# Taking the waits between indirect transfers out of a mixture-of-experts scatter and gather

## The reference

```python
probs = sigmoid(x @ router_w.T + expert_bias)      # 160 experts
top_w, top_idx = top_k(probs, 8)
top_w = 2.5 * top_w / (sum(top_w) + 1e-9)
h1 = silu(einsum('th,eih->eti', x, w_gate))         # 64 wide
routed = einsum('eti,ehi->th', h1 * combine.T[:, :, None], w_down)
out = routed + silu(x @ w_gate_shared.T) @ w_down_shared.T
```

## Time and profile before

| what | value |
|---|---|
| median of 3 runs | 2990.82 us (2987.16 to 2993.22) |
| profiled execution | 2990.82 us, of which the span of the core's instructions is 2989.0 us |
| PE busy | 1635.8 us, 55% |
| DVE busy | 1358.2 us, 45% |
| POOL busy | 1076.5 us, 36% |
| ACT busy | 951.4 us, 32% |
| granted TensorE clock, mean | 0.730 |
| moved by indirect transfers | 67.17 MB of 352.97 MB |

### The profile page before, as it was taken

The page is one execution under the profiler, slowest core; times in us unless marked ns, Lnnn a source line. Parts: engine busy times, 40 slices in busy tenths (PEclk is TensorE's granted clock), DMA queues, the critical chain, the costliest instruction groups (busy, mean ns, idle before and its releaser), DMA issues. The chain is left out here.

```text
span 2989.0 us, 40678 instructions
## 1 busy us (share of the span) xinstructions
PE 1635.8 (55%) x14020; PEld 1134.2 (38%) x14020; DVE 1358.2 (45%) x3644; ACT 951.4 (32%) x1757; POOL 1076.5 (36%) x1177
## 2 busy tenths in 40 slices
PE   3864411782555553355078445554313468888885
PEld 2543401562343443244056334342112333554454
DVE  3548820421223346667042112335433465766755
ACT  3641100331222241131033122222576532443444
POOL 1001555445444355565544454444551110000001
PEclk9985555896777765565579777676657776989998
DMA  8991112894666511211189656661110000000001
GB/s 235 260 397 48 37 40 81 294 327 148 215 205 205 180 50 38 57 39 38 43 270 327 209 185 212 191 210 58 38 37 11 1 1 1 2 1 2 1 2 29
DMA packets 276794, 352.97 MB, mean 118 GB/s; under 512 B 68625, under 2 KB 161105, under 8 KB 276433
## 3 DMA queue, kind: packets, MB, share of 16 engines
q10 hardware_dynamic: 83984, 153.13, 15.3%
q1 hardware_dynamic: 159840, 130.08, 14.6%
q0 software_dynamic: 32768, 67.17, 7.5%
HBM read 201.35 MB, written 167.51 MB: 123 GB/s over the span
## 5 line engine op out<-in xcount | busy, mean ns | idle before, releaser
L2033 POOL DMA_INDIRECT slot_rows<-arena,SLOTS x512 | 509.9, 996 | 558.1 <-DMA slot_rows<-arena,SLOTS 314.6
L2048 POOL DMA_INDIRECT arena<-slot_results,SLOTS x512 | 491.8, 961 | 525.6 <-issue 301.1
L1994 DVE COPY arena<-psum 128x512 f32<-128x512 f32 x288 | 194.5, 689 | 694.0 <-PE psum L2268 586.1
L2091 ACT ACTIVATE arena<-psum 128x512 f32<-128x512 f32 x288 | 171.9, 597 | 940.5 <-issue 384.4
L2219 PE MATMUL psum<-ident,arena 128*128 128x128 f32 x1152 | 222.7, 325 | 321.9 <-DMA arena<-slot_rows 321.9
L2268 PE MATMUL psum<-arena 64*128 64x128 f32 x2304 | 245.8, 341 | 259.3 <-DVE arena L1994 216.6
L2010 DVE SCALAR_TENSOR_TENSOR X<-arena,WEIGHTS,X 128x128 f32<-128x128 f32 x512 | 179.9, 352 | 355.4 <-DMA arena<-slot_results,SLOTS 339.2
L2268 PEld LDWEIGHTS psum<-arena 64*128 64x128 f32 x2304 | 184.6, 223 | 320.2 <-issue 289.1
L2219 PEld LDWEIGHTS psum<-ident,arena 128*128 128x128 f32 x1152 | 144.1, 161 | 365.5 <-issue 200.4
L2258 PE MATMUL psum<-arena 128*64 128x128 f32 x2304 | 219.0, 318 | 43.8 <-issue 43.0
L169 POOL TENSOR_SCALAR rstd<-mv 128x4 f32<-128x4 f32 x32 | 6.8, 212 | 610.0 <-DVE mv L581 609.7
(11 more groups left out here) (253 smaller groups left out, 3043.6 us busy)
## 6 DMA issues: line engine op xcount, KB each, us to landing
arena<-slot_rows ACTq DMA_DIRECT2D x288, 256.0 KB
slot_results<-arena ACTq DMA_DIRECT2D x288, 256.0 KB
arena<-expert_blocks SPq DMA_DIRECT2D x512, 96.0 KB
slot_rows<-zeros SPq DMA_DIRECT2D x2, 18432.0 KB, 80.0
arena<-own_blocks SPq DMA_DIRECT2D x44, 256.0 KB
slot_rows<-arena,SLOTS POOLq DMA_INDIRECT x512
arena<-slot_results,SLOTS POOLq DMA_INDIRECT x512
expert_blocks<-in_expert_w SPq DMA_DIRECT2D x1, 7680.0 KB, 26.1
```

Of the source, the lines that this page charges most:

```text
L1994: dve.tensor_copy(YSB[:, p].rearrange("p (c h) d -> p h c d", h=2), psum[:, first:first + 2, 0:256].rearrange("p h (c d) -> p h c d", c=2) ...
L2033: pool.indirect_dma_start(out=slot_rows[h], out_offset=bass.IndirectOffsetOnAxis(ap=slots_of(t, k), axis=0), in_=XNH[:, t], in_offset=None ...
L2048: pool.indirect_dma_start(out=GATHERED[:, n % TPI, k], out_offset=None, in_=slot_results[h], in_offset=bass.IndirectOffsetOnAxis(ap=slots_ ...
L2091: act.activation(XSBT[:, g % 2], psum[:, g % 2, :], ACT.Copy).then_inc(c_xt.sem, 1)
```

## The change

The four waits that pace POOL inside `dispatch` and `gather` are deleted. The waits for a tile's inputs stay (`e_xn`, `s_idx`, and `g_sum` for a free buffer), and so do the waits of ACT for a whole scatter, of POOL for all stores ahead of a gather, and of DVE for all 8 transfers of the tile that it sums.

```diff
             for t in range(HTILES * h, HTILES * h + HTILES):
                 pool.wait_ge(e_xn.sem, e_xn.at(run, t // TPI))
                 pool.wait_ge(s_idx.sem, s_idx.at(run, t // TPI))
-                if t % HTILES:
-                    pool.wait_ge(d_rows[h][(t - 1) % TPI].sem, d_rows[h][(t - 1) % TPI].at(run, (t - 1) % HTILES // TPI))
                 stand(pool)
                 for k in range(TOPK):
-                    if k == TOPK // 2:
-                        pool.wait_ge(d_rows[h][t % TPI].sem, d_rows[h][t % TPI].at(run, t % HTILES // TPI, 16 * k))
                     pool.indirect_dma_start(...)
...
             for n in range(HTILES * h, HTILES * h + HTILES):
                 pool.wait_ge(g_sum.sem, g_sum.at(run, n - TPI))
-                if n % HTILES:
-                    pool.wait_ge(g_rows[(n - 1) % TPI].sem, g_rows[(n - 1) % TPI].at(run, (n - 1) // TPI))
                 stand(pool)
                 for k in range(TOPK):
-                    if k == TOPK // 2:
-                        pool.wait_ge(g_rows[n % TPI].sem, g_rows[n % TPI].at(run, n // TPI, 16 * k))
                     pool.indirect_dma_start(...)
```

## The result

The kernel after takes 3177.22 us (median of 4 runs, 3172.23 to 3184.66), the kernel before 2990.13 (4 runs, 2987.16 to 2993.22): a ratio of 1.0628 [1.0602, 1.0653], 6.3% slower where 15% faster was forecast. The profiled execution took 3171.14 us, its span is 3169.2.

What follows compares the result with a forecast made beforehand. POOL's stream of indirect transfers, idling at the deleted waits, was taken to set the end. Stage gains summed to 462 us off a 2989.0 us span, giving 2527, or 2529 us with 1.8 around it; eight-in-ten range 2465 to 2730.

Steps and rivals of the forecast that it cites:

- The unit: Cost of one indirect transfer on POOL without the waits: 1.30 us a scatter, 1.26 us a gather.
- S1: First scatter stage, no expert stage beside it: 128 scatters would take 166.2 us; gain 51.5 us.
- E1, S2: First expert stage beside the second scatter stage: next expert loads could start after 201.5 us, not 258.3; gain 57.
- E2, G1: Second expert stage beside the first gather stage: 211 us instead of 287.5, DVE hardly waiting for gathers; gain 76.5.
- G2 and S3: Second gather and third scatter stages: third expert stage's loads 342 us after the gather stage's start, not 440; gain 98.
- E3, S4: Third expert stage beside the fourth scatter stage: 201.5 us instead of 259.3; gain 57.8.
- E4, G3: Fourth expert stage beside the third gather stage: 211 us instead of 286.6; gain 75.6.
- G4 and the rest: Last gather stage and mamba recurrence: ACT's three waits, 50.4 us, nearly vanish and ACT becomes the bound; gain 46.
- The third: Rival: DVE's work stretches packed transfers to 2.43 us each, making the kernel slower, 3503 us; chance 0.05.
- the long E1: Sign of being wrong: the first expert stage taking well over 200 us.
- The first: Rival: stages beside expert stages do not shrink because DMA backlog replaces the waits; 267 us lost, 2796 us; chance 0.15.
- The second: Rival: the wait moves into POOL's transfer instructions, which grow to the present pitch; nothing changes, 2991 us; chance 0.05.

Runs made afterwards that it cites:

- calm512_crowd768: Kernel after, plus POOL memsets before every second transfer: 512 elements in stages without an expert stage beside them, 768 in the others; 2631.92 us, ratio to before 0.8825.
- the memset part: Part of a kernel without the model: DVE and ACT pass a semaphore while POOL runs 96 memsets back to back; 1.17 us a round, 0.45 with POOL idle.
- hop: Kernel without the model: DVE and ACT pass a semaphore beside various POOL work; 1.40 us a round under scatters without waits, 0.47 with the waits of before.
- queue: Kernel without the model: DVE and ACT pass a token beside unpaced scatters, with extra copies or PE multiplies; delayed rounds 1.40 us, 7.00 with four more DVE copies.
- the ring: Kernel without the model: a token goes round DVE, ACT, PE and SP beside scatters with various pauses; 5.60 us a round without pauses, 0.76 with both landing waits.
- window4: Kernel after, with a wait before each transfer for the landing of the fourth one before it; 3152.62 us.

## Why the prediction was wrong

**The step that failed** is in "The unit": "waiting for landings only idles POOL", and with it the choice of 1.30 and 1.26 us for a transfer whatever stands beside it. I had named what the trace did not show, a run of more than eight transfers without a pause, and bounded it only by what it might do to POOL's own instructions. On them the bound held (980 and 956 ns). What it does to the others had no term in the sum. Shown: the small kernels have the delay with nothing changed but the pause (0.47 against 1.40 us), and pauses without any waits win the time back (2741 to 2632 us).

What it cost, term by term, between the same marks as in the prediction (first row loads of E1 to E4: 482.37, 810.78, 1582.43 and 1914.43 us in the kernel after; first transfers of G2 and G4: 1089.90 and 2194.95), in us gained; the last column is the best kernel of the experiments, calm512_crowd768 (484.08, 688.34, 1289.60, 1495.05; 906.56, 1712.20):

| term | forecast | after | calm512_crowd768 |
|---|---|---|---|
| S1 | 51.5 | 24 | 22 |
| E1, S2 | 57 | -70 | 54 |
| E2, G1 | 76.5 | 8 | 69 |
| G2 and S3 | 98 | -52 | 57 |
| E3, S4 | 57.8 | -73 | 54 |
| E4, G3 | 75.6 | 6 | 70 |
| G4 and the rest | 46 | -23 | 28 |
| sum | 462 | -180 | 354 |

**S1** took 168 us (166 forecast), but E1's loads start 28 us after its end, and S2's slot numbers were 54 us late; "Slot numbers and normalised rows come faster than that" rested on DVE's busy share of before, and a share of 0.41 says nothing when each PE step costs 20 us. **E1 | S2** and **E3 | S4** lost the most: 328 us from E1's loads to E2's, against 201.5 forecast, and not by 38 more scatters' DMA time (7 us) but by signals. **E2 | G1**: 279 us against 211, with DVE's 117.4 us gone as forecast and, for L1994, 106.1 us ahead of releases that the trace does not name (7.4 in the kernel before). **G2 and S3, E4 | G3** repeat this: the gaps before G3 and G4 are 120 and 47 us. **G4 and mamba**: G4 shrank by 31 us, and the time from the last gather to the end grew by 54; an idle time of 29.6 us of ACT ahead of such a release, at L1125, belongs to it.

**The rivals.** The third had the right sign at 0.05, by another mechanism: transfers stretched by DVE, where in fact DVE was held up by transfers; the means stayed at 0.98 and 0.96 us. Of the signs of being wrong that the prediction named, the long E1 is the one that came. The rule of the Trainium skill weighed there, SBUF — State Buffer, "SBUF: two separate sides", is seen in the memset part above, and not in the transfers' means. The first was right that crowded stages would not shrink by all that, with DMA backlog as the reason; the share of 0.21 in the stretch of E1 excludes it. The second did not occur.

**What the sum was worth once the pitch is right**: with pauses by time, at 1.50 us a transfer in the calm stages and 1.59 in the others where 1.30 and 1.26 had been forecast, the four terms of the expert stages come within 20 us of their forecast together, 247 of 267. The other 88 us that are missing lie in the terms of the calm stages, S1, G2 with S3, and G4. So most of the gain existed, but not by deleting the waits alone.

**Open.** What the transfers fill up is not shown, and so why a turn takes 1.40 us stays open. Once the delay is in, the trace itself holds fewer signals: in the kernel `hop`, part of scatters without waits, 0.8 of the transfers' 12.7 landing increments a microsecond (16 for each transfer), in the part with waits about 9 of 10.2. That would fit the path on which records of events leave the core; it is argued, not shown. The Trainium skill, NOTIFIC — the notification-queue block, "7.1 Overflow: three behaviours, one of which stalls the engine", says that the inner pipeline of this block holds back what feeds it rather than lose a record inside, and its "10. Constraints, capacities, measured rates" gives it room for some 500. By that rule the turns would belong to recording, and a run without it might not have them; the landing records that do go missing are not explained by it. Each run timed here comes with span and clock records of its own, so none can show it. The plain transfers, 30 landing increments a microsecond all recorded and no delay, speak against their number as the cause.

## What to carry to other kernels

A wait that looks idle may be spacing out something that others pay for: when a change lets an engine issue without pause, price what a long unbroken run does to the *other* engines, and if the trace has no such run, keep the range open there. When idle time ends in a release that has no instruction to it, compare the end of the producer with the start of the consumer; an engine that still waits 20 us and more after the work it needs was done waits for a signal's path, not for work. Here indirect transfers wanted a mean pitch of some 1.5 us (1.6 beside the expert stages), spread evenly, and such pauses by time gave more than waiting for landings did: 2632 against 2985 us.

## What the runs showed of the hardware

- Indirect transfers at a pitch of 1.264 us hold up DVE, ACT and PE (SP's share is not told apart) after 19 to 25 us where DVE and ACT have one instruction a round; scatters, gathers, and scatters of 32 rows do (`hop`: 1.40 us a round). Plain transfers on the same queue every 0.53 us do not (0.53 us a round, 0.45 alone).
- The delayed state is 1.40 us for each finished instruction, on each engine by itself (`queue`: 1.40 us for one copy a round, 7.00 for five, 2.80 for PE's multiply and weight load). Its onset came after some 10 us where DVE had five instructions a round. The limit of the mean pitch in the ring, between 1.39 and 1.46 us, is about that same turn.
- Landings of the transfers keep their time in S1: POOL, waiting in `window4` for the fourth one back, never paused more than 0.31 us there.
- A POOL memset of 1.11 us and a DVE copy of 8 elements run one after the other: 0.90 us for a copy that takes 0.17 alone.
